# Two entries from an MLP into the next attention: other places for chunk 1's query rotation and chunk 2's copies

## The reference, cut to what matters

```python
def _layer(x, wqkv, qs, ksc, wo, lg, lb, w1, b1, w2, b2):   # called twice
    h = shift_token(x)
    q, k, v = jnp.split(h @ wqkv, 3, axis=-1)                # 8 heads of 64
    q = l2norm(q) * qs
    k = l2norm(k) * ksc
    q, k = rotary_xpos(q, k)                                 # t*cos + rotate_half(t)*sin
    o = local_attention(q, k, v)      # chunks of 128 queries see their own and the chunk before
    x = x + o @ wo
    h = layer_norm(shift_token(x)) * lg + lb
    a, g = jnp.split(h @ w1 + b1, 2, axis=-1)
    return x + (a * gelu(g)) @ w2 + b2
x = _layernorm(x + attention_and_mlp_A(x))
x = _layernorm(x + two_layers(x))
```

## The kernel before, in words

| Name | What | Line of before |
|---|---|---|
| norms | sum of squares; maximum | L1290; L1296 |
| rotate, last add of q | DVE | L1459, L1462, L1463, L1302 |
| rotate_k | POOL | L1459, L1462, L1463, L2049 |
| scale_rotated | DVE, two | L1319 |
| tables; inverse_norms | POOL | L2038; L2055 |
| add_product; add_old | DVE | L1542; L1548 |
| finish_stats; finish | DVE | L1554, L1558, L1561; L1573 |
| k_t_low; q_t_low; h_low | DVE | L1323; L1328; L1284 |
| maxima; exponentials | DVE; ACT | L1344; L1837 |
| copy_qk; h_high | ACT | L1806, L1807; L1797 |
| scores; probabilities; rotated | PE | L875; L888; L849 |

## Time and profile before

### The profile page before, as it was taken

One profiled execution on the slowest core, in us unless ns is written; L12 is line 12 of the kernel. 1 busy time (PEld: TensorE's weight loads), 2 busy tenths in 40 slices (PEclk: granted clock), 3 DMA queues, 4 the chain that ended last, 5 costly groups with the idle time before them and its releaser, 6 DMA issues.

```text
span 1803.8 us, 43767 instructions
## 1 busy us (share of the span) xinstructions
PE 1736.5 (96%) x15424; PEld 1497.9 (83%) x15424; DVE 1496.1 (83%) x3797; ACT 1208.4 (67%) x3118; POOL 1066.8 (59%) x1030
## 2 busy tenths in 40 slices
PE   6999999989999899999999999989999999999997
PEld 5777777779999788888887888878888888878886
DVE  6898888868887889888897678788988889867776
ACT  6999999855444778787786343357877878743332
POOL 3566555443434677877775455467787777733343
PEclk9999999999999999999999999999999999999999
DMA  2111211022321211111112334231111111132221
GB/s 106 37 37 37 63 37 34 25 100 64 114 70 51 88 50 45 54 41 54 48 42 73 122 116 143 87 114 41 41 54 45 50 54 41 37 93 63 82 81 36
DMA packets 139813, 116.04 MB, mean 64 GB/s; under 512 B 10584, under 2 KB 138848, under 8 KB 138848
## 3 DMA queue, kind: packets, MB, share of 16 engines
q1 hardware_dynamic: 139616, 113.53, 20.2%
HBM read 75.74 MB, written 37.75 MB: 63 GB/s over the span
## 4 chain that ended last, share of the span: by engine, by line
PE 82%; DVE 8%; ACT 5%; issue 4%; POOL 0%; DMA 0%; SPq 0%; DVEq 0%; POOLq 0%; ACTq 0%
PE psum L567 17%; PE psum L569 17%; PE psum L568 17%; PE psum L907 6%; PE psum L875 5%; PE psum L888 5%; ACT a_probs L1719 4%; PE psum L663 3%; PE psum L849 3%; PE psum L653 2%; PE psum L681 2%; PE psum L921 2%; PE psum L621 2%; DVE psum L1208 1%; DVE a_neg_max L1210 1%
## 5 line engine op out<-in xcount | busy, mean ns | idle before, releaser
L1837 ACT ACTIVATE b_probs<-masked,neg_max 128x256 f32<-128x256 f32 (+1 forms) x512 | 250.1, 491 | 123.9 <-DVE neg_max L1344 123.9
L567 PE MATMUL psum<-wa_hi,b_h_hi 128*128 128x512 f32 (+1 forms) x576 | 233.8, 406 | 8.4 <-DVE wa_lo L1137 3.4
L1344 DVE CUSTOM_DVE_ANT_0 masked<-psum,mask 128x256 f32<-128x256 f32 (+1 forms) x512 | 177.3, 412 | 75.5 <-PE psum L875 75.5
L569 PE MATMUL psum<-wa_hi,b_h_lo 128*128 128x512 f32 (+1 forms) x576 | 214.7, 373 | 0.0
L568 PE MATMUL psum<-wa_lo,b_h_hi 128*128 128x512 f32 (+1 forms) x576 | 214.3, 372 | 0.0
L567 PE MATMUL psum<-g_h_hi,wm_hi 128*128 128x512 f32 (+1 forms) x480 | 190.5, 397 | 3.2 <-POOL g_h_lo L2106 1.7
L2055 POOL TENSOR_TENSOR g_in<-g_in,minus_half 128x16 f32<-128x16 f32 x64 | 187.9, 2936 | 4.5 <-DVE g_in L1296 4.5
L569 PE MATMUL psum<-g_h_hi,wm_lo 128*128 128x512 f32 (+1 forms) x480 | 189.3, 394 | 0.0
L568 PE MATMUL psum<-g_h_lo,wm_hi 128*128 128x512 f32 (+1 forms) x480 | 189.3, 394 | 0.0
L1459 POOL TENSOR_TENSOR g_in<-g_z,g_in 128x512 f32<-128x512 f32 x62 | 79.8, 1286 | 143.6 <-DVE g_in L1290 138.4
L567 PE MATMUL psum<-wm_hi,u_hi 128*128 128x256 f32 x576 | 164.3, 285 | 0.1
(11 more groups left out here) (168 smaller groups left out, 5606.5 us busy)
## 6 DMA issues: line engine op xcount, KB each, us to landing
x_mid<-y_out SPq DMA_DIRECT2D x96, 128.0 KB, 1.7
rope_in<-in_rope SPq DMA_DIRECT2D x64, 128.0 KB, 2.2
x_res<-x_state SPq DMA_DIRECT2D x64, 128.0 KB, 2.4
g_in<-x_mid SPq DMA_DIRECT2D x32, 256.0 KB, 3.7
g_old<-x_state SPq DMA_DIRECT2D x16, 512.0 KB, 4.0
out_x<-g_fin SPq DMA_DIRECT2D x15, 512.0 KB, 3.0
w_raw<-in_w_mlp_b SPq DMA_DIRECT2D x2, 2154.0 KB, 9.5
x_in<-in_x SPq DMA_DIRECT2D x32, 128.0 KB, 2.2
```

Source lines behind the costliest of these rows:

```text
L567: nc.tensor.matmul(out, a_hi, b_hi, start=first, stop=False)
L569: return nc.tensor.matmul(out, a_lo, b_hi, start=False, stop=last)
L1344: ins = nc.vector.tensor_tensor_reduce(out[:, at], src[:, at], (mask if now else mask0)[:, at], -1.0, BIG, ALU.add, ALU.min, neg_max[:, r, ...
L1837: ins = nc.scalar.activation(out, src, ACT.Exp, bias=neg_max[:, r, k:k + 1], scale=-1.0, accum_out=row_sum[:, n % 2, 4 * r + k:4 * r + k + 1])
```

## The change

In both entries, and nowhere else, work is put in another order. No instruction is added or taken away.

- DVE, opening 3: `scale_rotated(0)` goes ahead of `norms(1, 1)`, and `rotate_q(1)` is done here, ahead of `add_product` half 1, no longer in step 0.
- DVE, steps -1 and 0: of `finish_stats` only the first part (`finish_parts`, four BN_STATS) stays in step -1; the second (`finish_variance`) goes behind `scale_rotated(1)`. `norms(2, ...)` and `h_low(3)` stand around it, ahead of `finish` and `copy_probs`; `k_t_low(1)` goes between the two `copy_probs`.
- ACT, step 0: `copy_qk(2, ...)` and `h_high(3)` stand between the two rounds of chunk 0's exponentials; `k_t_high(1)` and `q_t_high(1)` go ahead of `copy_probs(0, 1)`.
- PE, step 0: `transpose_rotated(1, ...)` and `project_v(2)` go ahead of `transpose_probs(0, 1)`.
- POOL, step 0: `tables(2)` goes ahead of the final norm's power.

```diff
@@ PE, step loop
                 if s == 0:
-                    transpose_probs(s, 0)
+                    transpose_probs(0, 0)
+                    transpose_rotated(1, 1)
+                    transpose_rotated(1, 0)
+                    project_v(2)
...
-                if b_chunk(s + 1):
+                if b_chunk(s + 1) and s != 0:
                     transpose_rotated(s + 1, 1)
                     transpose_rotated(s + 1, 0)
...
-                if b_chunk(s + 2):
+                if b_chunk(s + 2) and s != 0:
                     project_v(s + 2)
@@ DVE, opening 3
             if opening == 3:
+                scale_rotated(0)
                 norms(1, 1)
-                scale_rotated(0)
                 norms(1, 0)
+                rotate_q(1)
                 return
@@ DVE, step loop
-                if b_chunk(s + 1) and s + 1 > 0:
+                if b_chunk(s + 1) and s + 1 > 1:
                     rotate_q(s + 1)
                 if s == 0:
-                    scale_rotated(s + 1)
-                    h_low(s + 3)
+                    scale_rotated(1)
+                    dve_mlp(..., opening="finish_variance")
+                    norms(2, 1)
+                    h_low(3)
+                    norms(2, 0)
                     dve_mlp(..., opening="finish")
...
-                if b_chunk(s + 2) and s + 2 > 1:
+                if s == 0:
+                    k_t_low(1)
+                elif b_chunk(s + 2) and s + 2 > 1:
                     norms(s + 2, 1)
                 if b_chunk(s):
                     copy_probs(s, 1)
-                if b_chunk(s + 2) and s + 2 > 1:
+                if b_chunk(s + 2) and s + 2 > 2:
                     norms(s + 2, 0)
...
                 if s == -1:
                     h_low(2)
-                    dve_mlp(..., opening="finish_stats")
+                    dve_mlp(..., opening="finish_parts")
@@ ACT, step loop
+                if s == 0:
+                    copy_qk(2, 1)
+                    copy_qk(2, 0)
+                    h_high(3)
                 if b_chunk(s):
                     exponentials(s, 1)
...
+                if s == 0:
+                    k_t_high(1)
+                    q_t_high(1)
                 if b_chunk(s):
                     copy_probs(s, 1)
@@ POOL, step loop
                 if s == 0:
+                    tables(2)
                     pool_mlp(..., opening="finish")
```

More of the change, by code:

```diff
@@ L1403, in dve_attention @@
                     add_residual(s - 2)
-                if b_chunk(s + 1) and s + 1 > 0:
+                if b_chunk(s + 1) and s + 1 > 1:
                     rotate_q(s + 1)
                 if s == 0:
-                    scale_rotated(s + 1)
-                    h_low(s + 3)
+                    scale_rotated(1)
+                    dve_mlp(v, *mlp_behind(layer), None if layer == 0 else layer - 1, opening="finish_variance")
+                    norms(2, 1)
+                    h_low(3)
+                    norms(2, 0)
                     dve_mlp(v, *mlp_behind(layer), None if layer == 0 else layer - 1, opening="finish")
@@ L1434, in dve_attention @@
                 if b_chunk(s + 1):
-                    k_t_low(s + 1)
+                    if s != 0:
+                        k_t_low(s + 1)
                     q_t_low(s + 1)
@@ L1438, in dve_attention @@
                     h_low(2)
-                    dve_mlp(v, *mlp_behind(layer), None if layer == 0 else layer - 1, opening="finish_stats")
+                    dve_mlp(v, *mlp_behind(layer), None if layer == 0 else layer - 1, opening="finish_parts")
                 if b_chunk(s - 2) and s not in (NCH - 2, NCH - 1):
@@ L1551, in finish_stats, with finish_parts @@
             def finish_stats(t, slot, at=slice(0, 4), more=0):
+                finish_parts(t, slot, at, more)
+                finish_variance(t, at, more)
+            def finish_parts(t, slot, at=slice(0, 4), more=0):
                 v.wait_ge(S["f_sum"], t + 1 + more)
@@ L1555, in finish_stats, with finish_variance @@
                 ins.then_inc(S["f_stats"], 1)
+            def finish_variance(t, at=slice(0, 4), more=0):
                 v.wait_ge(S["f_stats"], t * 2 + 1 + 2 * more)
@@ L1631, in dve_mlp @@
                 h_low(base)
-            if opening == "finish_stats":
-                finish_stats(base + NGRP - 1, 1)
+            if opening == "finish_parts":
+                finish_parts(base + NGRP - 1, 1)
+            if opening == "finish_variance":
+                finish_variance(base + NGRP - 1)
             if opening == "finish":
@@ L1882, in act_attention @@
                     copy_spread(s - 1)
+                if s == 0:
+                    copy_qk(2, 1)
+                    copy_qk(2, 0)
+                    h_high(3)
                 if b_chunk(s):
                     exponentials(s, 1)
-                if s == 0:
-                    h_high(s + 3)
-                if b_chunk(s + 2) and s + 2 > 1:
+                if b_chunk(s + 2) and s + 2 > 2:
                     copy_qk(s + 2, 1)
```

## The result

The kernel before took 1805.53 us (median of 8 runs, 1804.28 to 1807.22), the changed one 1811.13 us (8 runs, 1808.98 to 1812.7). The ratio is 1.0028, with a 95% interval of 1.0018 to 1.0038: 5.6 us slower, where 6.0 were forecast. The profiled execution of the changed kernel took 1811.06 us around a span of 1809.3, 5.5 us more than before.

The account below looks back on a forecast made before the run. DVE's row from the MLP's last sums to `q_t_low(1)` was taken to bound both entries. Layer 0: 1.1 + 0.7 - 0.4 = +1.4; layer 1: 3.9 + 0.7 = +4.6; +6.0 on 1805.48 gives 1811.5 us, 8-in-10 range 1802.2 to 1814.9.

Parts of the forecast that it names:

- The rotation beside POOL's: Opening 3: DVE's and POOL's rotations take 5.9 us together; last sums 2.05 us late in layer 0, 4.95 in layer 1.
- the alternation: DVE's and POOL's instructions with both inputs in SBUF take turns one by one, four of each in opening 3.
- Ahead of the maxima: Shorter `add_old` and moved variance save 0.41 + 0.55 us in layer 0, 0.52 + 0.55 in layer 1.
- T: The end of chunk 0's maxima on DVE, forecast to move +1.1 us in layer 0 and +3.9 in layer 1.
- From T to q_t_low(1): DVE's row behind chunk 0's maxima takes 10.0 us, 0.7 longer than before, as `finish` falls into POOL's rotation.
- The clock, and step 1: Low clock falls elsewhere, 0.4 us won in layer 0; DVE's row of step 1 behind it left alone.
- The terms of contention: Delays up to `q_t_low(1)` from DVE and POOL meeting: +1.1 and +0.7 us in layer 0, +4.6 in layer 1.
- Rival 1: No turns: DVE's pieces, once they have the lock, run in a row; -1.0 us, 1804.5 us; chance 0.17.
- Rival 2: The rotations hardly disturb each other, DVE's under 2.5 us in opening 3; -3.9 us, 1801.7 us; chance 0.12.
- Rival 3: PE's waits in layer 1 bring two more low-clock stretches of 3.4 us, half of each lost; 1814.9 us; chance 0.13.
- the lock as the prediction states it: DVE and POOL share an SBUF port pair under an exclusive lock, held for the whole of an instruction.

Follow-up runs that it names:

- e3: The changed kernel with POOL's rotation of chunk 1's keys held until DVE's rotation of the queries is through: 1808.99 us (kernel before 1805.45), ratio 1.0023.
- e6: The changed kernel with the variance ahead of the maxima and `finish` ahead of the norms releasing POOL's next rotation: 1806.21 us (kernel before 1804.46), ratio 1.0004.
- e7: The changed kernel with ten extra matmuls, results overwritten, where PE waits ahead of chunk 1's scores: 1808.45 us (kernel before 1804.46), ratio 1.0023.
- e10: The changed kernel with e6's order and e3's wait in both entries: 1802.62 us (kernel before 1805.24), ratio 0.9984.
- e2: The changed kernel with opening 3's rotation and scaling put back, so step 0's new order alone: 1812.89 us (kernel before 1805.45), ratio 1.0041.
- e4: The kernel before with the whole change in layer 0's entry only: 1807.88 us (kernel before 1805.45), ratio 1.0014.
- e9: The kernel before with the changed order, e6's order and e3's wait in layer 0's entry only: 1802.21 us (kernel before 1805.24), ratio 0.9989.

## Why the prediction was right, step by step

**The rotation beside POOL's.** Right in kind. The prediction had it last until 9.3 us behind the event (582.5 - 573.19); in layer 0 the last sums start 8.74 behind it, in layer 1 8.15. Against before that is +1.48 and +4.29, where +2.05 and +4.95 were forecast. POOL's start was as computed (3.43 us behind the event, forecast 3.41), but the eight pieces took 5.3 us and not 5.9. DVE's first add started right behind the small maximum, before POOL's second, and a POOL piece beside one of DVE's short halves grew by 0.2 us (0.91 for 0.73), not by the half's whole 0.35. So the alternation holds, but the sum of all durations is its upper bound here. (In the earlier trace rows the four instructions of `finish` stood beside three of POOL's, so "each waited for one of POOL's" was said too strongly.) e3 confirms the mechanism by its absence, 2.0 us for the rotation.

**Ahead of the maxima.** `add_old` at 1.23 and the moved variance gave what they should, and 0.3 us more in layer 0 and 0.1 in layer 1. In layer 0 half of that is the wait for ACT's high part of chunk 0's keys behind `add_old`, 0.17 us before and now gone; in both layers the variance took up 0.67 us of the row and not 0.55. T moved by +0.24 and +3.08 us; +1.1 and +3.9 were forecast.

**From T to q_t_low(1).** Forecast 10.0 us; it is 9.56 in layer 0 (586.16 to 595.72), before 9.31. `h_low(3)` waited for ACT, 0.55 us; `finish` took 2.88 where about 3 was forecast. It ended at T + 7.63, not T + 8.0. +0.25 against +0.7. e6 confirms the cause: out of POOL's way, `finish` takes 1.38.

**The clock, and step 1.** This is the term that was wrong in sign. I took 0.4 us as won in layer 0; the maxima of chunk 1 start 1.79 us behind `q_t_low(1)` and not 1.56, so 0.23 were lost. And I called DVE's row of step 1 untouched: it is so in the program, but PE at half clock brought chunk 1's probabilities late, for which DVE waited 0.85 and 0.70 us. Before, that wait was 0.22 and none. With it, step 1 cost 0.64 us more in layer 0 and 0.82 in layer 1. e7 shows that this is the clock's doing, for with a full clock behind `q_t_low(1)` the wait falls to 0.28 us in layer 0 and to nothing in layer 1.

**So the sum was right in its mechanism and lucky in its size: two errors cancel.** The terms of contention were together 1.3 us too large in layer 0 (1.1 + 0.7 forecast, 0.24 + 0.25 found) and 1.3 in layer 1 (4.6; 3.08 + 0.24); the clock was 0.63 and step 1 0.64 too small in layer 0, and step 1 0.82 in layer 1. The total is 5.5 in the entries for 6.0.

**The rivals.** Rival 1, DVE's pieces in a row, is excluded by the rotation: one of POOL's stands between each two of the rotation's four. (What the prediction says "the second rival turns on", who comes next when both wait, is what this first rival turns on.) Rival 2, rotations that hardly disturb each other, needed under 2.5 us for DVE's; it was 4.1 (575.53 to 579.67). Rival 3, two more low stretches in layer 1 with 3.4 us lost, was half right: there was one stretch more at each entry and not two in layer 1, and by e7 the one behind `q_t_low(1)` costs 0.8 us in layer 1 and 0.9 to 1.3 in layer 0. Not foreseen: POOL's copy of the inverse row sums waited 5.89 us in layer 0, by the profile for the DMA of the zero row. In e10 that wait is 0.88 us; no run separates what it costs, and DVE's row did not wait for it here.

**What stays open.** Where the 7.4 us of e2 come from in full: its two entries account for 5.3. Its profiled execution, at 1810.97 us, was only 5.4 above before's, so the entries explain that one and not what the other runs have beyond it. Why layer 0 has 2.4 us by e4's times and 1.4 or 0.5 by two profiles: single profiles of this kernel differ by 1 to 2 us in parts that a change leaves alone, beside low stretches of the clock that fall differently. And a run with DVE's order of e6 but without any meeting of the scaling and `tables(2)` in layer 1, where in e10 1.82 for 1.29 us is still lost, wasn't tried. Nor did any run have the new order of PE, ACT or POOL in step 0 by itself: that these cost nothing, as the prediction says, is argued. e6, e9 and e10 keep them, and what they may cost is within those kernels' times.

## What to carry to other kernels

Before moving DVE work like this rotation or this `finish` into a gap, read POOL's row at the same time: the two rotations side by side took nearly the sum of both (5.3 of 5.9 us), and the gap is only worth its length if POOL is quiet or made to wait. Finishing the norm before POOL's next rotation, and nothing else, made the difference between slower by 0.28% and no measurable change. And a late engine can be paid for twice: PE waits, its clock falls, and the next step, which nobody touched, starts late.

## What the runs showed of the hardware

- DVE's maximum over 16 columns, alone 0.17 us (e10 at 577.10), took 0.86 when started inside one of POOL's multiplications (the changed kernel, 574.75 and 574.29). So a small instruction can wait as long as a large one.
- Not everything waits. The sum of squares took 0.67 us inside POOL's first multiplication (before, DVE at 595.09, POOL from 595.01 to 596.28), as it does alone. And the MLP's last sums, which read one operand from PSUM, took 0.74 us for two between POOL's first and last piece of the rotation, and 0.74 in the changed kernel beside POOL's power. The Trainium skill, "SBUF — State Buffer", section "SBUF: two separate sides", counts DVE instructions with two SBUF inputs, or in a two-port mode, among those that lock; the rotation, which waits, and these sums, which don't, agree.
- POOL's power over 16 columns, 2.9 to 3.9 us long, does not hold DVE for its length: in layer 0 of the changed kernel it runs from 579.09 to 582.44, and `add_old`, which reads two SBUF operands, took 1.23 us inside it (1.22 in the earlier trace rows). The next one there runs from 599.46 to 602.37, and the whole rotation of chunk 2's queries went through inside it at 0.69, 0.42, 0.42 and 0.69 us. So the lock as the prediction states it, held for the whole of an instruction, is not what these rows show for the power.
